# Expert choice one step every other unit, the count at unit 100, scatters two units apart from unit 116

## The chip, the cores and the metric

The kernel runs on one core of one Trainium2 chip. The metric is the device time of one execution in microseconds. TensorE (PE), VectorE (DVE), ScalarE (ACT) and GpSimd (POOL) work side by side and wait for each other through semaphores; SyncE (SP) issues most transfers.

## The reference, cut to what matters

Sixteen images of 128 channels by 1024 positions go through an attention layer and a mixture-of-experts layer:

```
x = x + attention(layernorm_over_channels(x))      # 8 heads of 16, 1024 x 1024 scores per head
t = tokens(x)                                      # 16 x 1024 tokens of 128
t = t + experts(layernorm(t))                      # 16 experts, 128 -> 512 -> 128, two per token
```

The gating takes, per token, a softmax over 16 logits and the two largest gates with their experts. An expert takes at most 256 tokens of an image by its first mask and, behind those, tokens of the second mask. This needs a running count of tokens per expert over the image (`cumsum`) and gives every token two places in the experts' lists. Each chosen token is scaled by its gate and summed.

## The kernel before, in words

**Two phases.** The first runs over the 16 images (the code's batches, `B`): attention, and for the image before it the projection, the residual, the layer norm, the gating and the scatter of its rows, sorted by expert, to `sorted_rows` in memory. The second runs over 136 x 2 blocks of 128 sorted rows: the experts. Only the first is touched here.

**Units.** A batch is 128 units (`SLOTS`), each one 128 x 512 tile of exponentials, in four stages of 32 (`UNITS`). In unit `u` PE makes a tile of scores for the maxima of unit `u + 45` (`max_unit`, L1405, matmul L1415), then the tile of scores of unit `u` (`score_unit`, L1429, matmul L1439). At u mod 32 = 2, 7, 10, 14, 18, 22, 26 and 30 it also weighs the values with four tiles of exponentials (`weigh`, L1443, eight matmul records of L1456). DVE reduces the first tile to its row maxima (`take_max`, L946, L952), ACT takes the exponentials of the second (L795). Both kinds of tile have three buffers (`RING = 3`), so that PE is at most three tiles ahead of DVE and of ACT.

**Side work** is written out by unit number in each engine's program; an engine runs its program in order. DVE: `divide` in units 4 to 7 of each stage (L977), norm statistics in units 8 to 17 and 24 to 32, residual additions at 13 and 17, the start of the gating at 38 (`choose`), and then `choose_experts` (L1040), a generator of 22 steps: one is taken after `take_max` of each unit from 44 on, left out where u mod 32 is in `BUSY` (3 to 7 and 18 to 21). So before the change the steps stand in units 44 to 49, 54 to 66 and 72 to 74. The twentieth step also writes `masks_b` (L1103), which PE's `count_tokens` (L1484, 16 small matmuls) waits for. PE counts at unit 77 and ACT copies the counts at unit 78 (`copy_counts`, L845).

**POOL** runs, in this order within batch b: the last scatters of image b-2, with `place_v(b, 1)` (L584) behind the first of them; `normalise_x(b+1)` (L567), whose result PE needs for `project_qk` (L1391) at unit 33; `normalise_tokens(b-1)`; `split_qk`, `place_v(b+1, 0)` and `add_bias`; `place_rows(b-1)` (L615), which waits for the counts and for all 22 steps of the choice; and the first scatters of image b-1 (`scatter`, L721, one indirect transfer of 128 rows, L732, which waits for the score tile of its unit).

Of the kernel before, what the change touches and what calls it, by code (L numbers as in the profile page):

```python
# [25 lines left out]
UNITS = TB * HG  # L26
# [6 lines left out]
BUSY = (3, 4, 5, 6, 7, 18, 19, 20, 21)  # L33
# [66 lines left out]
def metaformer(nc, x, wq, wk, wv, wproj, bproj, wgate, w1, w2, out):  # L100
    ctx = ExitStack()
    with ctx:
# [34 lines left out]
        at = 0  # L137
# [374 lines left out]
        def _(gp):  # L512
# [227 lines left out]

            def batch(b, first, last):
                at = SLOTS * b
                rest = range(8, 16) if b > 1 else range(0)
                for n in rest[:1]:
                    scatter(b - 2, n, at + 1)
                place_v(b, 1)
                for n in rest[1:5]:
                    scatter(b - 2, n, at + 4 * (n - 8) + 1)
                if not last:
                    normalise_x(b + 1)  # L750
                for n in rest[5:]:
                    scatter(b - 2, n, at + 4 * (n - 8) + 1)
                if not first:
                    normalise_tokens(b - 1)
                if not last:
                    for i in range(4):
                        split_qk(b + 1, i)
                    place_v(b + 1, 0)
                add_bias(b)
                if not first:  # L760
                    place_rows(b - 1)
                    if b == EARLY:
                        keep_counts()
                    for n in range(16 if last else 8):
                        scatter(b - 1, n, at + 96 + (2 if last else 4) * n)

            for b in range(B):
                batch(b, b == 0, b == B - 1)
# [20 lines left out]
        def _(act):  # L789
# [68 lines left out]
            def batch(b, first, last):  # L858
                for u in range(SLOTS):
                    exp_unit(b, u)  # L860
                    if not last:
                        if u == 2:
                            copy_xt(b + 1, 0)
                        if u == 6:
                            copy_xt(b + 1, 1)
                        if u == 33:
                            copy_qk(b + 1, 0)
                        if u == 42:
                            copy_qk(b + 1, 1)
                        if u == 45:  # L870
                            copy_qk(b + 1, 2)
                        if u == 49:
                            copy_qk(b + 1, 3)
                        if u == 52:
                            copy_v(b + 1, 0)
                        if u == 55:
                            copy_v(b + 1, 1)
                    if not first:
                        if u == 21:
                            copy_tokens(b - 1, 0)  # L880
                        if u == 23:
                            copy_tokens(b - 1, 1)
                        if u == 41:
                            gate_exponentials(b - 1)
                        if u in (74, 82):
                            copy_rows(b - 1, (u - 74) // 8)
                        if u == 78:
                            copy_counts(b - 1)
                    if u % UNITS == MSLOT + 1 and not (last and u > 96):
                        copy_m(b, u // UNITS + 1)  # L890
# [54 lines left out]
        def _(dve):  # L945
# [215 lines left out]
            def batch(b, first, last):  # L1161
                for u in range(SLOTS):
# [14 lines left out]
                    if not first:  # L1177
# [10 lines left out]

                        if u == 44:
                            choice = choose_experts(b - 1)  # L1190
                        if u >= 44 and u % UNITS not in BUSY:
                            next(choice, None)

            batch(0, True, False)
# [180 lines left out]
        def _(pe):  # L1375
# [138 lines left out]
            def batch(b, first, last):  # L1514
                freed[0] = (m_copied, STAGES * b + 1)
                for u in range(SLOTS):
# [25 lines left out]
                    if not first:  # L1542
# [7 lines left out]
                            transpose_tokens(b - 1, 1)  # L1550
                        if u == 36:
                            logits(b - 1)
                        if u == 77:
                            count_tokens(b - 1)
                    if u % UNITS == MSLOT and not (last and u > 96):
                        rows_of_maxima(b, u // UNITS + 1)
# [106 lines left out]
```

## Time and profile before

| | us |
|---|---|
| three runs | 2384.68, 2387.88, 2392.95 |
| median | 2387.88 |
| profiled execution, its own time | 2377.1 |
| its span, first to last instruction | 2375.2 |
| first phase, 16 batches, ends near | 1741 |
| a batch, from unit 0 to unit 0 | 104.9 to 106.5 |

The engines' busy shares are over the whole span, and the first phase is where the change is. A reader finds the time of a unit by counting the records of L952 (DVE) or L795 (ACT): record 128 b + u of L795 is unit u of batch b, and record 128 b + u + 45 of L952. For batch 6, which the rows are taken from, this gives the start of DVE's unit 44 at 731.9 us, 58 at 745.6, 67 at 752.6, 72 at 756.7, 80 at 763.0, 100 at 776.7, 107 at 782.5 and 112 at 785.8, and ACT's unit 0 at 691.9 and of the next batch at 796.8. A line of a timeline can merge neighbours (x4: four in a row, with their time from the first start to the last end).

### The profile page before, as it was taken

The page shows a single profiled execution, that of the slowest core. Times are in us where ns is not written, and L with a number is a line of the kernel's source. Part 1 is how long each engine was busy: PE and PEld are TensorE (multiplying, and loading weights), DVE is VectorE, ACT ScalarE, POOL GpSimd, SP SyncE. Part 2 cuts the span into 40 slices and gives each one's busy share as a digit, 9 for nine tenths or more (in the row PEclk, how much of TensorE's full clock was granted, in tenths as well). Part 3 has the DMA queues.
Part 4 walks back from the last instruction along what each step waited for, and adds up shares of the span by engine and source line. Part 5 has one row for each costly group of instructions (what it writes and reads, how often), then busy time and mean ns, then how long its engine had stood idle before and what let it go on. Part 6 is the DMA issues. An engine that isn't in the chain of part 4 may idle for free. (4 is left out here: it accounts for less than half of the span.)

```text
span 2375.2 us, 49241 instructions
## 1 busy us (share of the span) xinstructions
PE 2119.9 (89%) x14610; PEld 1161.0 (49%) x14610; DVE 1846.1 (78%) x4351; ACT 1542.5 (65%) x3153; POOL 1041.2 (44%) x1630
## 2 busy tenths in 40 slices
PE   6999999898999999899999999999846999999994
PEld 3333333333333333333333333333326999999994
DVE  6898989989998999999899998999733554445573
ACT  1677777767677777767777777777723665556551
POOL 3204544443444445344444434444344555555542
PEclk9999999999999999999999999999968999999997
DMA  4223323132323323232332313223052222222684
GB/s 121 46 41 59 62 49 72 35 66 48 64 57 57 68 41 68 41 63 53 65 62 49 70 36 65 54 53 63 17 181 72 70 70 67 67 70 70 177 248 133
DMA packets 134693, 170.57 MB, mean 72 GB/s; under 512 B 31118, under 2 KB 101140, under 8 KB 134450
## 3 DMA queue, kind: packets, MB, share of 16 engines
q1 hardware_dynamic: 117618, 134.24, 26.4%
q0 software_dynamic: 16896, 34.12, 4.1%
q8 instruction: 90, 1.47, 0.3%
q14 instruction: 89, 0.73, 0.1%
HBM read 64.86 MB, written 48.86 MB: 48 GB/s over the span
## 5 line engine op out<-in xcount | busy, mean ns | idle before, releaser
L952 DVE TENSOR_REDUCE sb_m_red<-banks 128x1 f32<-128x512 f32 x2048 | 1325.9, 678 | 152.4 <-PE banks L1415 144.1
L795 ACT ACTIVATE sb_arena_a<-banks 128x512 f32<-128x512 f32 x2048 | 1115.3, 599 | 446.4 <-PE banks L1439 406.8
L1415 PE MATMUL banks<-sb_arena_b 62*128 62x512 f32 x2048 | 814.4, 467 | 105.1 <-DVE sb_m_red L952 91.2
L1439 PE MATMUL banks<-sb_arena_b 64*128 64x512 f32 x2048 | 806.4, 462 | 10.7 <-ACT sb_arena_a L795 5.7
L1415 PEld LDWEIGHTS banks<-sb_arena_b 62*128 62x128 f32 x2048 | 346.9, 187 | 769.8 <-DVE sb_m_red L952 637.3
L1456 PE MATMUL banks<-sb_arena_a,sb_arena_d 128*32 128x512 f32 x4096 | 550.7, 610 | 10.0 <-ACT sb_arena_a L795 4.2
L732 POOL DMA_INDIRECT sorted_rows<-sb_rows,sb_place x256 | 251.2, 981 | 341.3 <-PE banks L1439 306.2
L778 POOL DMA_INDIRECT expert_out<-sb_arena_d x272 | 274.2, 1008 | 268.5 <-DVE sb_arena_d L1321 178.6
L1439 PEld LDWEIGHTS banks<-sb_arena_b 64*128 64x128 f32 x2048 | 337.8, 185 | 32.0 <-ACT sb_arena_a L795 24.6
L1584 PE MATMUL banks<-sb_arena_d,sb_arena_c 128*128 128x128 f32 x2176 | 289.4, 276 | 1.3 <-ACT sb_arena_d L908 1.3
L1593 PE MATMUL banks<-sb_arena_c 128*128 128x128 f32 x2176 | 287.9, 275 | 2.6 <-ACT sb_arena_c L915 1.7
L1314 DVE COPY sb_arena_c<-sb_arena_b 128x512 f32 x272 | 141.0, 518 | 173.1 <-issue 95.5
L1584 PEld LDWEIGHTS banks<-sb_arena_d,sb_arena_c 128*128 128x128 f32 x2176 | 265.9, 193 | 2.2 <-issue 1.7
L1593 PEld LDWEIGHTS banks<-sb_arena_c 128*128 128x128 f32 x2176 | 264.8, 192 | 3.7 <-issue 2.8
L915 ACT ACTIVATE sb_arena_c<-banks 128x512 f32<-128x512 f32 x272 | 162.5, 598 | 108.4 <-PE banks L1584 95.9
L1311 DVE COPY sb_arena_c<-sb_arena_a 128x512 f32 x272 | 114.2, 420 | 88.5 <-PE banks L1584 55.0
L922 ACT ACTIVATE sb_arena_d<-banks,sb_arena_d 128x128 f32<-128x128 f32 x272 | 100.1, 368 | 108.4 <-issue 55.0
L1456 PEld LDWEIGHTS banks<-sb_arena_a,sb_arena_d 128*32 128x32 f32 x4096 | 80.8, 108 | 155.0 <-issue 73.6
L588 POOL TENSOR_SCALAR sb_arena_d<-sb_v_st 128x512 f32<-128x512 f32 x32 | 19.8, 619 | 272.9 <-PE banks L1456 256.2
L1576 PE MATMUL banks<-sb_ident,sb_arena_d 128*128 128x128 f32 x272 | 74.7, 274 | 32.2 <-DMA sb_arena_d<-sorted_rows 32.2
L908 ACT ACTIVATE sb_arena_d<-banks 128x128 f32<-128x128 f32 x272 | 74.1, 272 | 42.8 <-PE banks L1576 39.4
L1395 PE MATMUL banks<-sb_xt,sb_wq_r 128*128 128x512 f32 x128 | 76.0, 677 | 10.2 <-POOL sb_xt L570 8.1
(185 smaller groups left out, 1617.3 us busy)
## 6 DMA issues: line engine op xcount, KB each, us to landing
sb_arena_b<-sb_arena_c SPq DMA_DIRECT2D x768, 64.0 KB, 2.3
sb_arena_d<-sorted_rows SPq DMA_DIRECT2D x272, 66.0 KB
sb_x_in<-in_x_dram SPq DMA_DIRECT2D x16, 512.0 KB, 3.8
sb_res<-in_x_dram SPq DMA_DIRECT2D x16, 512.0 KB, 3.6
sb_x_all<-sb_res SPq DMA_DIRECT2D x16, 512.0 KB, 3.1
expert_out<-sb_arena_d POOLq DMA_INDIRECT x272
sorted_rows<-sb_rows,sb_place POOLq DMA_INDIRECT x256
sb_arena_a<-in_L_ffn_w_dram SPq DMA_DIRECT2D x1, 4096.0 KB, 14.0
```

The costliest lines, as they stand in the source:

```text
L732: nc.gpsimd.indirect_dma_start(out=sorted_rows[:, :], out_offset=bass.IndirectOffsetOnAxis(ap=place[:, k, j:j + 1], axis=0), in_=rows[:, k ...
L778: nc.gpsimd.indirect_dma_start(out=expert_out[:, :], out_offset=bass.IndirectOffsetOnAxis(ap=blk_dest[:, s % WR:s % WR + 1], axis=0), in_= ...
L795: nc.scalar.activation(probs[:, u % PRING, :], ps_score[:, u % RING, :], ACT.Exp, scale=SCALE).then_inc(exp_done, 1)
L915: nc.scalar.activation(hid[:, s % 2, :], ps_h[:, s % 2, :], ACT.Relu).then_inc(hid_done, 1)
L952: nc.vector.tensor_reduce(out=m_red[:, s % 2, at:at + 1], in_=ps_max[:, m % SLOTS % RING, :], axis=AX.X, op=ALU.max).then_inc(max_taken, 1)
L1311: nc.vector.tensor_copy(w1_blk[:, s % WR, :], w1_all[:, bass.ds(e, 1), :].rearrange("p a h -> p (a h)")).then_inc(w1_copied, 1)
L1314: nc.vector.tensor_copy(w2_blk[:, s % WR, :], w2_all[:, bass.ds(e, 1), :, :].rearrange("p a c d -> p (a c d)")).then_inc(w2_copied, 1)
L1415: nc.tensor.matmul(ps_max[:, m % SLOTS % RING, :], qs[rows_of, g, l, half * HALF + t * P:half * HALF + (t + 1) * P], ks[rows_of, g, l, kh ...
L1439: nc.tensor.matmul(ps_score[:, u % RING, :], ks[rows_of, g, l, i * P:(i + 1) * P], qs[rows_of, g, l, half * HALF:(half + 1) * HALF], start ...
L1456: last = nc.tensor.matmul(ps_pv[32 * h:32 * h + 32, :], v_pad[:, i, HG * g + h, :], probs[:, (4 * n + h) % PRING, :], start=(i == 0), stop ...
L1584: last = nc.tensor.matmul(ps_h[:, s % 2, c * P:(c + 1) * P], w1_blk[:, s % WR, c * P:(c + 1) * P], blk_xt[:, s % 2, :], start=True, stop=True)
L1593: last = nc.tensor.matmul(ps_o[s % WR], hid[:, s % 2, c * P:(c + 1) * P], w2_blk[:, s % WR, c * P:(c + 1) * P], start=(c == 0), stop=(c == ...
```

## The change

The choice takes one step in odd units alone: 45, 47, 49, 55, 57, 59, 61, 63, 65, 73, 75, 77, 79, 81, 87, 89, 91, 93, 95, 97, 105 and 107, the twentieth at 97. The count moves to unit 100 on PE and its copy to 101 on ACT. Of an image's 16 scatters six instead of eight are written behind `place_rows`, from unit 116 on two units apart (before: eight from 96 on, four apart), and ten in the next batch in units 1 to 19, two apart (before: eight in units 1 to 29, four apart); all ten now stand before `normalise_x`, of which before three stood behind it. The last batch keeps its choice in every unit, its count at 77 and its sixteen scatters from 96.

```diff
-                rest = range(8, 16) if b > 1 else range(0)
+                rest = range(6, 16) if b > 1 else range(0)
                 for n in rest[:1]:
                     scatter(b - 2, n, at + 1)
                 place_v(b, 1)
-                for n in rest[1:5]:
-                    scatter(b - 2, n, at + 4 * (n - 8) + 1)
+                for n in rest[1:]:
+                    scatter(b - 2, n, at + 2 * (n - 6) + 1)
                 if not last:
                     normalise_x(b + 1)
-                for n in rest[5:]:
-                    scatter(b - 2, n, at + 4 * (n - 8) + 1)
...
-                    for n in range(16 if last else 8):
-                        scatter(b - 1, n, at + 96 + (2 if last else 4) * n)
+                    for n in range(16 if last else 6):
+                        scatter(b - 1, n, at + (96 if last else 116) + 2 * n)
...
-                        if u == 78:
+                        if u == (78 if last else 101):
                             copy_counts(b - 1)
...
-                        if u >= 44 and u % UNITS not in BUSY:
+                        if u >= 44 and (u % 2 or last) and u % UNITS not in BUSY:
                             next(choice, None)
...
-                        if u == 77:
+                        if u == (77 if last else 100):
                             count_tokens(b - 1)
```

## Rows read from the trace of the kernel before

**Rows 1.** The page's line of busy times.

```profile
PE 2119.9 (89%) x14610; PEld 1161.0 (49%) x14610; DVE 1846.1 (78%) x4351; ACT 1542.5 (65%) x3153; POOL 1041.2 (44%) x1630
```

**Rows 2.** Windows: stretch, length, busy us of PE, PEld, DVE, ACT, POOL, granted clock.

```profile
269.50:375.40 105.90, 97.28 (x616) 38.17 (x616) 96.04 (x216) 77.04 (x147) 47.97 (x86) 0.98 0.29 57
587.10:692.00 104.90, 95.88 (x616) 37.79 (x616) 96.09 (x216) 77.14 (x147) 47.99 (x86) 1.00 0.28 57
...
303.10:306.40 3.30, 3.30 (x16) 0.99 (x14) 3.05 (x8) 1.57 (x3) 3.22 (x7) 0.50 0.52 166
```

**Rows 3.** Windows of batch 6: units 44 to 57, 58 to 66, 72 to 79, 80 to 99.

```profile
731.90:745.60 13.70, 12.73 (x84) 5.29 (x82) 11.28 (x28) 9.76 (x20) 4.95 (x5) 1.00 0.00 1
745.60:752.60 7.00, 6.18 (x42) 2.28 (x38) 7.00 (x19) 5.21 (x11) 0.51 (x1) 1.00 0.18 30
...
756.70:763.00 6.30, 6.03 (x48) 2.54 (x48) 5.37 (x13) 4.78 (x11) 0.76 (x2) 1.00 0.40 68
763.00:776.70 13.70, 12.56 (x84) 4.48 (x84) 12.67 (x24) 11.43 (x24) 10.22 (x37) 1.00 0.29 49
```

**Rows 4.** Timeline of DVE, batch 6, units 59 and 60, then the steps of 65 and 66.

```profile
746.46 0.69 DVE L952 TENSOR_REDUCE sb_m_red<-banks 128x1 f32<-128x512 f32 x1
747.07 0.28 DVE L1067 TENSOR_TENSOR sb_tmp<-sb_gat,sb_small 128x128 f32<-128x128 f32 x1
747.27 0.68 DVE L952 TENSOR_REDUCE sb_m_red<-banks 128x1 f32<-128x512 f32 x1
...
751.67 0.16 DVE L1097 TENSOR_TENSOR sb_masks<-sb_masks,sb_small 128x8 f32<-128x8 f32 x1
...
752.35 0.38 DVE L1100 TENSOR_TENSOR sb_masks<-sb_masks,sb_small 128x8 f32<-128x8 f32 x1
```

**Rows 5.** Timeline of DVE from unit 111: no choice there; in brackets idle time, releaser.

```profile
785.25 2.48 DVE L952 TENSOR_REDUCE sb_m_red<-banks 128x1 f32<-128x512 f32 x4 [0.22 <-PE banks L1415]
...
793.53 2.48 DVE L952 TENSOR_REDUCE sb_m_red<-banks 128x1 f32<-128x512 f32 x4 [0.38 <-PE banks L1415]
```

**Rows 6.** Timeline of PE over the same units.

```profile
786.00 0.49 PE L1415 MATMUL banks<-sb_arena_b 62*128 62x512 f32 x1 [0.30 <-DVE sb_m_red L952]
...
786.42 1.06 PE L1456 MATMUL banks<-sb_arena_a,sb_arena_d 128*32 128x512 f32 x8
...
788.70 0.50 PE L1415 MATMUL banks<-sb_arena_b 62*128 62x512 f32 x1 [0.30 <-DVE sb_m_red L952]
```

**Rows 7.** Timeline of PE around the count at unit 77.

```profile
759.02 0.49 PE L1415 MATMUL banks<-sb_arena_b 62*128 62x512 f32 x1
...
760.49 0.50 PE L1415 MATMUL banks<-sb_arena_b 62*128 62x512 f32 x1
```

**Rows 8.** Timeline of DVE, units 78 and 79, behind that count.

```profile
761.03 0.69 DVE L952 TENSOR_REDUCE sb_m_red<-banks 128x1 f32<-128x512 f32 x1 [0.20 <-PE banks L1415]
762.45 1.29 DVE L952 TENSOR_REDUCE sb_m_red<-banks 128x1 f32<-128x512 f32 x2 [0.73 <-PE banks L1415]
```

**Rows 9.** Timeline: PE's scores of units 100 and 101, then DVE's maximum of unit 101.

```profile
775.93 0.61 PE L1415 MATMUL banks<-sb_arena_b 62*128 62x512 f32 x2
...
777.96 0.65 DVE L952 TENSOR_REDUCE sb_m_red<-banks 128x1 f32<-128x512 f32 x1
```

**Rows 10.** Timeline of POOL: first and last of the 36 instructions of `place_rows`.

```profile
762.16 0.46 POOL L635 TENSOR_TENSOR sb_tmp<-sb_counts,sb_masks 128x128 f32<-128x128 f32 x1 [7.10 <-ACT sb_counts L848]
...
774.28 0.20 POOL L676 CAST sb_place<-sb_small 128x16 int32<-128x16 f32 x1
```

**Rows 11.** Timeline of POOL: first and last of sixteen scatters with nothing between them.

```profile
1775.63 1.11 POOL L732 DMA_INDIRECT sorted_rows<-sb_rows,sb_place  x1 [0.54 <-POOL sb_place L718]
...
1795.10 0.96 POOL L732 DMA_INDIRECT sorted_rows<-sb_rows,sb_place  x1 [0.30 <-issue]
```

**Rows 12.** Timeline, batch 6: `normalise_x` on POOL, then the first `project_qk` on PE.

```profile
708.47 0.20 POOL L558 TENSOR_SCALAR sb_ln_var<-sb_mean_var 128x8 f32<-128x8 f32 x1 [1.56 <-DVE sb_mean_var L1005]
...
710.82 3.48 POOL L570 TENSOR_SCALAR sb_xt<-sb_xt,sb_neg_mean,sb_rstd 128x128 f32<-128x128 f32 x8
...
720.21 1.12 PE L1395 MATMUL banks<-sb_xt,sb_wq_r 128*128 128x512 f32 x2
```

## The prediction

> **What bounds the kernel now.** First read the line of busy times [rows 1]: PE 89% and DVE 78% over the span. These are averages over two phases, and the change touches only the attention phase, so the windows of whole batches come next [rows 2]. In a batch of 104.90 us PE is busy 95.88 and DVE 96.09. Neither is the bound alone: both have about 9 us of idle time, not at the same places. The question is where a DVE step lies beside a busy PE (it is free) and where beside an idle one (it costs).
>
> The windows by units answer it [rows 3]. In units 44 to 57 DVE is busy 11.28 of 13.70 us and PE 12.73: PE has the projections of the next image there, and DVE waits for it. In units 58 to 66 DVE is busy 7.00 of 7.00 us and PE 6.18: DVE is the bound, with a choice step in every unit. In units 72 to 79 DVE is busy 5.37 of 6.30 and PE 6.03: the count stops DVE. In units 80 to 99 DVE is busy 12.67 of 13.70.
>
> The timeline gives the prices. Back to back, the maxima come 0.60 us apart: four in 2.48 us with 0.68 for the last [rows 4, 5], (2.48 - 0.68) / 3 = 0.60. With one step of 0.28 us between, they come 747.27 - 746.46 = 0.81 us apart, since neighbours overlap [rows 4]. So such a step costs DVE 0.20. Where there are no steps, four units still take 788.70 - 786.00 = 2.70 us, not 2.40 [rows 6]. That is a loop: PE makes a tile, DVE reduces it, that frees one of three buffers, PE makes a tile (0.49), weighs (1.06) and only then makes the next. Once per four units PE waits 0.30 for DVE [rows 6] and DVE waits 0.22 for PE [rows 5]. DVE's work in a group is 0.69 + 3 x 0.60 = 2.49, so 0.21 is spare, and 0.09 more comes back when DVE no longer waits (its first maximum then takes 0.60, not 0.69). One step of 0.20 in four units is free. Two make 2.40 + 0.40 = 2.80 us, 0.10 above the loop. Four make 3.20, 0.50 above it. This is the whole case for spreading: a steeper price for dense steps.
>
> **Units 44 to 57, five steps fewer.** PE is the bound; a lighter DVE waits longer for the same tiles. Gain 0. The cover is PE's 12.73 busy us in 13.70 [rows 3].
>
> **Units 58 to 66, nine steps become four.** Now 7.00 us [rows 3]. After: unit 58 without a step 0.60, units 59 to 62 with two steps 2.80, units 63 to 66 with two, one of them smaller, 2.74. Sum 6.14, 0.86 less. But DVE now reaches unit 67, behind the weighing of unit 66, without arrears and meets the wait of the loop, 0.22 + 0.09 = 0.3. Gain 0.56, say 0.6; bounds 0.3 (the wait is as long as the 0.38 of another group [rows 5] and the groups take 2.9) and 0.9 (no wait). Here the profile also shows two engines in each other's way: the step L1100 takes 0.38 us beside POOL's `place_v`, while L1097, of the same shape, takes 0.16 [rows 4]. The step moves to unit 95, where POOL is idle; its 0.2 is within the 0.6. The Trainium skill (GPSIMD Engine Reference, Specifications) says that GpSimd shares its SBUF interfaces with VectorE and contends with DVE instructions that have two SBUF inputs, and the trace agrees, with these 0.38 and 0.16 us. By that rule `place_rows`, now beside units 107 to 126, could slow other DVE steps; they are few and I add nothing.
>
> **Units 72 to 79, three steps become four and the count leaves.** Now 6.30 to 6.38 us. Behind the count DVE waits 0.20 and 0.73 [rows 8]. After, four steps on eight units: 8 x 0.60 + 4 x 0.20 = 5.60. Gain 0.75; bounds 0.5 (one wait of the loop stays) and 0.8.
>
> **Units 80 to 107, nine steps come in.** Steps of 0.20 at 81 and 87, 0.14 at 89, 0.08 at 91, 93, 95 and 105, about 0.34 at 97 (with the cast for the count) and 0.10 at 107: 1.3 us of DVE time. There are five groups up to 99, one weighing each, with 0.31 spare each, and 0.31 in the last group before 112. By groups only 84 to 87 is over, by 0.1 to 0.15. Cost 0.15; bounds 0 and 1.3 (nothing is hidden).
>
> **The count at unit 100.** It holds up PE: the next tile comes 760.49 - 759.02 = 1.47 us after the last instead of some 0.4, so it costs PE about 1.05 us [rows 7]. At unit 100 DVE starts the four steps of `divide`. PE's tile of unit 100 starts at 775.93; with the count behind it the next would start at 777.40 and be done at 777.89, and DVE asks for it at 777.96 [rows 9]. So the count is just covered, by the transpose that DVE makes before. ACT's copy of 0.5 us behind it sits in an engine that is busy 77 of 105 us [rows 2]. The masks are written at DVE's unit 97, before PE may be at 100 (three buffers). Cost 0; bounds 0 and 0.93, what DVE waits behind it now [rows 8]. I take 0 because the times above say so, without much to spare.
>
> **POOL and what is queued behind its waits.** `place_rows` waits for the 22nd step, now in unit 107 at 782.6 + 0.2, instead of at 762.16; it takes 774.48 - 762.16 = 12.3 us [rows 10] and ends at about 795.1, that is 1.7 us before the next unit 0 at 796.8 and 10 units behind unit 116. So the scatters will not follow the written spacing: they run back to back. Sixteen such take (1795.10 - 1775.63) / 15 = 1.30 us each [rows 11]. From 795.7 on (a start 0.5 to 0.8 behind) they take 16 x 1.30 = 20.8, with `place_v` (0.8) between: to 817.3, or 20.5 us behind unit 0. Only then `normalise_x` starts, which takes 710.82 + 3.48 - 708.47 = 5.8 us [rows 12]: ready at 26.3 us. PE asks for it at 720.21 - 691.9 = 28.3 us [rows 12]. It is covered, with 2.0 us to spare where there were 5.9. `place_v(b, 1)` is late by 6 us for a use at unit 71. The first `project_qk`, the tiles behind it on PE, and through them DVE and ACT, all wait if that margin goes. SP's queue waits for none of these.
>
> **The sum.** 0.6 + 0.75 - 0.15 - 0 = 1.2 us a batch. The choice is changed in 14 batches (1 to 14): 14 x 1.2 = 16.8 us. The profiled execution, 2377.1 us, would take 2360.3. It is 10.8 us under the median of the runs shown; the same 16.8 off the median 2387.88 gives 2371.1. Bounds of the terms: best 0.9 + 0.8 = 1.7 a batch, 24 us, 2364; the ordinary bad side 0.3 + 0.6 - 0.4 = 0.5 a batch, 7 us, 2381.
>
> **Rivals.**
> (a) The steps cost what they take and the count is not covered. The 9 steps cost, say, 0.7 instead of 0.15 and the count gives back 0.5: 0.6 + 0.75 - 0.7 - 0.5 = 0.15 a batch, 2 us, 2386. For it: the cover of the count is 0.07 us by the rows. Against it: 0.31 spare per group is measured, and behind unit 103 DVE is behind anyway.
> (b) POOL is late. If the scatters beside running attention take more than 1.30 + 2.0 / 16 = 1.43 us each, or `place_rows` starts 2 us later, PE stops at unit 33 in every batch, and all of the lateness is lost, since PE is the bound there. From 3.2 us of lateness (a scatter of 1.50 us) the gain is gone; at 1.6 us a scatter, 4.8 us late, 2.8 are lost: 14 x (2.8 - 1.2) = 22 us slower, 2410. For it: one spacing in the middle of the phase, right behind `place_rows`, was 1.4. Against it: the other close ones were 1.3, as in the tail.
> (c) The clock. TensorE's granted clock fell to half (1.2 GHz) five times in the phase, as at 303.1 [rows 2], each time in units 35 to 38, behind small matmuls of the logits among waits; such a batch took 105.9 instead of 104.9. PE then does the same kind of work at 100 (small count matmuls, then waits for DVE). If the clock fell there in each batch, 14 x 1.0 = 14 us would eat the gain: 2385. The Trainium skill (TensorE: Matmul & The Clock Gate, Part 1) says that the clock is gated by how busy PE has been; at unit 77, where the count is now, no fall is seen.
> (d) The written spacing of scatters does nothing, since POOL runs behind it (above). That is part of the forecast, not against it.
>
> **How the numbers follow.** Forecast 2371, its own range 2362 to 2381, chance 0.72. (a) 0.14, (c) 0.04, both about no change; (b) 0.10, of which 0.07 slower by over 0.3% and 0.03 a smaller loss. The range for 8 in 10 takes in part of (a) and (c): 2362 to 2387. 0.3% is 7.2 us, about what a measurement of this kernel tells from no change: faster 0.73, same 0.18, slower 0.09.
>
> **What would show it.** In the profile after: batches of 103.7 us; units 58 to 66 in about 6.2 us and 72 to 79 in about 5.6; units 80 to 99 no longer than 13.9; no DVE wait over 0.3 behind the count; the sixteen scatters back to back with `normalise_x` ending near 26 us after unit 0 and no wait of L1395 for it. A wait of L1395 for POOL, or a DVE wait of 0.5 or more at unit 101, would make me wrong.

## The result and the profile after

The change made the kernel slower. The median of four runs is 2492.73 us (2490.30 to 2494.37), the kernel before beside it 2388.08 (2384.68 to 2392.95, four runs); the ratio is 1.0447 with a 95% interval of 1.0421 to 1.0474. The profiled execution took 2493.6 us, its span is 2491.7. The forecast was 2371, faster. Of the experiments below, two executions of v2_dense (3240 and 4672 us) and one of x1_rows16 (6675 us) took far longer than the rest for a reason that no profile shows; their figures leave these out.

Lines of the text from L760 on stand two lower than in the kernel before: the maximum is L950, its matmul L1413, the scores L1437, the weighing L1454, the exponentials L793. In the kernels with added transfers on GpSimd the maximum is L967 and the scores L1454.

The page after; under the busy line the fortieths of the span, for TensorE's granted clock in tenths. It answers to [rows 1].

```profile
span 2491.7 us, 49241 instructions
...
PE 2187.5 (88%) x14610; PEld 1182.8 (47%) x14610; DVE 1835.9 (74%) x4351; ACT 1533.1 (62%) x3153; POOL 1037.8 (42%) x1630
...
PEclk9999899999989998989999999989876999999997
```

PE is 68 us busier with the same 14610 matmuls, and the clock, which in the kernel before fell to half five times for 3.4 us in the attention phase, now falls near the head of every batch from batch 2 on, for 6.8 to 13.7 us. That says that something is different in each batch, not what.

Windows of after (stretch, length, busy us of PE, PEld, DVE, ACT, POOL, granted clock): batch 5 whole, then of batch 6 the units 0 to 15, 44 to 57, 58 to 66, 72 to 79 and 80 to 99. They answer to [rows 2, 3].

```profile
606.90:718.30 111.40, 98.52 (x616) 38.49 (x616) 95.79 (x215) 76.90 (x148) 47.65 (x86) 0.95 0.26 54
...
718.40:741.80 23.40, 18.33 (x85) 7.63 (x86) 14.08 (x31) 10.03 (x19) 14.20 (x16) 0.71 0.37 76
...
767.00:780.70 13.70, 12.73 (x84) 5.29 (x82) 10.13 (x23) 9.76 (x20) 4.96 (x5) 1.00 0.01 1
780.70:787.10 6.40, 5.99 (x40) 2.03 (x36) 6.23 (x14) 4.93 (x10) 0.29 (x1) 1.00 0.14 24
791.10:796.80 5.70, 5.18 (x34) 1.68 (x34) 5.67 (x13) 4.61 (x10) 0.00 (x0) 1.00 0.45 76
796.80:810.50 13.70, 13.01 (x87) 4.59 (x88) 13.59 (x32) 11.37 (x23) 0.00 (x0) 1.00 0.29 49
```

The same units 0 to 15 in the kernel before:

```profile
692.00:706.60 14.60, 13.61 (x85) 5.92 (x86) 13.53 (x31) 10.41 (x20) 5.01 (x6) 1.00 0.43 75
```

Every window that the forecast spoke of came out near it: 7.00 became 6.40, 6.30 became 5.70, 13.70 stayed 13.70. The loss is in units 0 to 15, which it did not price: 14.60 became 23.40. Of these 8.8 us, 4.1 are more idle time of PE (5.07 against 0.99) and 4.7 more busy time, at a clock of 0.71. DVE and ACT do the same work in more time. Over batches 2 to 13 the mean is 14.6 before and 23.1 after; a batch takes 112.7 instead of 105.3, and 14 times 7.4 (batches 2 to 15) is 104 us, the whole difference.

Now the timelines of that stretch in batch 6, whose unit 0 is at 718.4. First POOL; between the second line shown and the `place_v` at 726.78 stand five more scatters, 1.26 us apart.

```profile
718.06 1.11 POOL L732 DMA_INDIRECT sorted_rows<-sb_rows,sb_place  x1 [0.80 <-issue]
719.48 0.97 POOL L732 DMA_INDIRECT sorted_rows<-sb_rows,sb_place  x1 [0.30 <-issue]
...
726.78 0.63 POOL L588 TENSOR_SCALAR sb_arena_d<-sb_v_st 128x512 f32<-128x512 f32 x1
727.60 0.99 POOL L732 DMA_INDIRECT sorted_rows<-sb_rows,sb_place  x1 [0.18 <-remote]
728.90 0.95 POOL L732 DMA_INDIRECT sorted_rows<-sb_rows,sb_place  x1 [0.30 <-issue]
732.16 0.95 POOL L732 DMA_INDIRECT sorted_rows<-sb_rows,sb_place  x1 [2.31 <-remote]
```

Then DVE, PE and ACT.

```profile
719.99 0.69 DVE L950 TENSOR_REDUCE sb_m_red<-banks 128x1 f32<-128x512 f32 x1 [0.34 <-PE banks L1413]
721.41 0.69 DVE L950 TENSOR_REDUCE sb_m_red<-banks 128x1 f32<-128x512 f32 x1 [0.73 <-issue]
723.84 0.69 DVE L950 TENSOR_REDUCE sb_m_red<-banks 128x1 f32<-128x512 f32 x1 [1.73 <-PE banks L1413]
...
726.08 0.69 DVE L950 TENSOR_REDUCE sb_m_red<-banks 128x1 f32<-128x512 f32 x1 [0.93 <-PE banks L1413]
...
731.88 0.69 DVE L950 TENSOR_REDUCE sb_m_red<-banks 128x1 f32<-128x512 f32 x1 [4.96 <-remote]
```

```profile
721.22 0.63 PE L1413 MATMUL banks<-sb_arena_b 62*128 62x512 f32 x2
...
722.37 0.50 PE L1413 MATMUL banks<-sb_arena_b 62*128 62x512 f32 x1
...
724.58 0.79 PE L1413 MATMUL banks<-sb_arena_b 62*128 62x512 f32 x1 [1.14 <-DVE sb_m_red L950]
...
727.78 0.79 PE L1413 MATMUL banks<-sb_arena_b 62*128 62x512 f32 x1
...
732.63 0.79 PE L1413 MATMUL banks<-sb_arena_b 62*128 62x512 f32 x1 [3.67 <-issue]
```

```profile
727.51 0.60 ACT L793 ACTIVATE sb_arena_a<-banks 128x512 f32<-128x512 f32 x1 [2.37 <-remote]
731.92 0.60 ACT L793 ACTIVATE sb_arena_a<-banks 128x512 f32<-128x512 f32 x1 [3.81 <-remote]
```

DVE is idle though PE's tiles are recorded long before. PE's three tiles from 721.22 to 722.87 are taken at 723.84, 726.08 and 731.88: the last is 9.0 us late. ACT waits at the same times for the other kind of tile. The packed trace also records steps of the semaphore that PE raises for DVE, though not every one: the last before these three starts are at 723.81, 726.05 and 731.86, each within 0.03 us of the start. So DVE starts as soon as its signal is there, and it is the signal that comes late. It is a circle: PE has three buffers and can't go on until DVE frees one, so PE waits as well (1.14, 3.67), its clock falls, and a tile of 0.50 takes 0.79. The longer waits of DVE begin at the fourth scatter (722.1) and behind the seventh (726.9), and the engines go on some two us after the run pauses at 729.85, because POOL itself then waits for the score tile of a unit that is held up (2.31). "remote" as a releaser means that a semaphore step is recorded where the wait ends, but no instruction's record ends near it; "issue" means that not even a step is shown. Here "remote" is the sign that a signal came later than the work it stands for.

So the sixteen scatters do not run back to back from first to last. In batch 6 nine follow each other closely, with `place_v` between the seventh and the eighth; then the engines that they held up make POOL itself wait, and the last ends at 744.19, 26.1 us behind the start of the first. The pattern is the same in each batch from 2 to 15, with nine to twelve close ones.

### The profile page after: what moved, and what is told of

It is laid out like the page before. It is cut to its first block and busy times, and to the rows that moved or that the text cites. A ratio compares the mean times of both kernels' runs of the same rounds, so it can differ in the third digit from the quotient of the medians.

```text
span 2491.7 us, 49241 instructions
## 1 busy us (share of the span) xinstructions
PE 2187.5 (88%) x14610; PEld 1182.8 (47%) x14610; DVE 1835.9 (74%) x4351; ACT 1533.1 (62%) x3153; POOL 1037.8 (42%) x1630
## 3 DMA queue, kind: packets, MB, share of 16 engines
q0 software_dynamic: 16896, 34.12, 3.9%
q8 instruction: 90, 1.47, 0.2%
## 5 line engine op out<-in xcount | busy, mean ns | idle before, releaser
L950 DVE TENSOR_REDUCE sb_m_red<-banks 128x1 f32<-128x512 f32 x2048 | 1331.4, 679 | 252.2 <-PE banks L1413 169.9
L793 ACT ACTIVATE sb_arena_a<-banks 128x512 f32<-128x512 f32 x2048 | 1113.6, 599 | 559.0 <-PE banks L1437 442.7
L1413 PE MATMUL banks<-sb_arena_b 62*128 62x512 f32 x2048 | 830.5, 477 | 141.8 <-DVE sb_m_red L950 103.7
L1437 PE MATMUL banks<-sb_arena_b 64*128 64x512 f32 x2048 | 824.9, 474 | 22.3 <-issue 11.2
L1413 PEld LDWEIGHTS banks<-sb_arena_b 62*128 62x128 f32 x2048 | 352.7, 192 | 825.2 <-DVE sb_m_red L950 655.8
L1454 PE MATMUL banks<-sb_arena_a,sb_arena_d 128*32 128x512 f32 x4096 | 570.3, 630 | 5.1 <-ACT sb_arena_a L793 1.7
L1437 PEld LDWEIGHTS banks<-sb_arena_b 64*128 64x128 f32 x2048 | 343.8, 190 | 56.2 <-ACT sb_arena_a L793 32.6
L1312 DVE COPY sb_arena_c<-sb_arena_b 128x512 f32 x272 | 131.4, 483 | 187.8 <-PE banks L1591 128.8
L635 POOL TENSOR_TENSOR sb_tmp<-sb_counts,sb_masks 128x128 f32<-128x128 f32 x15 | 6.9, 457 | 414.2 <-DVE sb_small L1110 387.3
L1454 PEld LDWEIGHTS banks<-sb_arena_a,sb_arena_d 128*32 128x32 f32 x4096 | 81.8, 109 | 155.0 <-issue 78.4
L588 POOL TENSOR_SCALAR sb_arena_d<-sb_v_st 128x512 f32<-128x512 f32 x32 | 20.1, 629 | 242.0 <-PE banks L1454 224.8
```

The lines of the kernel that those rows point to most:

```text
L793: nc.scalar.activation(probs[:, u % PRING, :], ps_score[:, u % RING, :], ACT.Exp, scale=SCALE).then_inc(exp_done, 1)
L950: nc.vector.tensor_reduce(out=m_red[:, s % 2, at:at + 1], in_=ps_max[:, m % SLOTS % RING, :], axis=AX.X, op=ALU.max).then_inc(max_taken, 1)
L1312: nc.vector.tensor_copy(w2_blk[:, s % WR, :], w2_all[:, bass.ds(e, 1), :, :].rearrange("p a c d -> p (a c d)")).then_inc(w2_copied, 1)
L1413: nc.tensor.matmul(ps_max[:, m % SLOTS % RING, :], qs[rows_of, g, l, half * HALF + t * P:half * HALF + (t + 1) * P], ks[rows_of, g, l, kh ...
L1437: nc.tensor.matmul(ps_score[:, u % RING, :], ks[rows_of, g, l, i * P:(i + 1) * P], qs[rows_of, g, l, half * HALF:(half + 1) * HALF], start ...
L1454: last = nc.tensor.matmul(ps_pv[32 * h:32 * h + 32, :], v_pad[:, i, HG * g + h, :], probs[:, (4 * n + h) % PRING, :], start=(i == 0), stop ...
```

## The experiments

What follows separates the theories: that the dense run of scatters as such holds PE up (in the expectations, theory D, for density), or its place (P), the choice and the count (C), the bytes in memory (Y), GpSimd's making of descriptors, the records that tell the DMA engines what to move (G), or the form of the transfer. The gain or loss by stretch is the mean over batches 2 to 13 of DVE's time by units, against the kernel before.

### One half of the change at a time

**s1_spacing**, the new places of the scatters with the old choice and count:

```diff
-                rest = range(8, 16) if b > 1 else range(0)
+                rest = range(6, 16) if b > 1 else range(0)
...
-                for n in rest[1:5]:
-                    scatter(b - 2, n, at + 4 * (n - 8) + 1)
+                for n in rest[1:]:
+                    scatter(b - 2, n, at + 2 * (n - 6) + 1)
...
-                for n in rest[5:]:
-                    scatter(b - 2, n, at + 4 * (n - 8) + 1)
...
-                    for n in range(16 if last else 8):
-                        scatter(b - 1, n, at + 96 + (2 if last else 4) * n)
+                    for n in range(16 if last else 6):
+                        scatter(b - 1, n, at + (96 if last else 116) + 2 * n)
```

> The kernel before with the scatter edit alone: six from unit 116 and ten in units 1 to 19, two units apart, with the choice and the count where they were. Place_rows ends at unit 97, so the scatters follow their units: 1.36 us apart before unit 0 and 1.7 us behind it, not back to back. Theory D (scatters back to back for more than some 5 us hold up PE): little or no stall, 2380 to 2400 us. Theory P (any dense scatters in units 1 to 12, where the stack moves and the transposes lie, hold up PE): a stall of several us a batch, 2450 us or more. Theory C (the moved choice and count do it): 2388 us.

Measured: 2408.73 us against 2379.28, ratio 1.0126 (1.0063 to 1.0189). The scatters are on time here, yet units 120 to 127 take 1.2 us more, 0 to 7 1.15 and 8 to 15 0.35. Two units apart is some 1.8 us on average, but in bursts of up to six neighbours at 1.3. So the written spacing of two alone costs 1%, less than a third of the loss. That is more than theory D allowed for (2400 at most) and far below theory P's 2450.

**s3_choice**, the new choice, count and copy with the scatters where the kernel before has them; against the changed kernel:

```diff
-                rest = range(6, 16) if b > 1 else range(0)
+                rest = range(8, 16) if b > 1 else range(0)
...
-                for n in rest[1:]:
-                    scatter(b - 2, n, at + 2 * (n - 6) + 1)
+                for n in rest[1:5]:
+                    scatter(b - 2, n, at + 4 * (n - 8) + 1)
...
+                for n in rest[5:]:
+                    scatter(b - 2, n, at + 4 * (n - 8) + 1)
...
-                    for n in range(16 if last else 6):
-                        scatter(b - 1, n, at + (96 if last else 116) + 2 * n)
+                    for n in range(16 if last else 8):
+                        scatter(b - 1, n, at + 96 + (2 if last else 4) * n)
```

> The changed kernel with the scatter schedule of before. Place_rows still ends near unit 126, so eight scatters run back to back from there to about unit 9, and eight follow four units apart. Theory D: a part of the stall, 2 to 4 us a batch, less 1.2 us that the choice gains: 2400 to 2430 us. Theory P: about the same as D. Theory C: 2490 us.

Measured: 2479.34 us against 2379.28, ratio 1.0423 (1.0361 to 1.0484). The late choice alone brings nearly the whole loss, since eight scatters that were written from unit 96 on find `place_rows` unfinished and are caught up on in one run across unit 0. Units 0 to 15 take 8.8 us more; units 56 to 63, 64 to 71 and 72 to 79 take 0.33, 0.32 and 0.70 less, as in the full change. Theory D's range, 2400 to 2430, was missed, and theory C's 2490 came nearer; the next two runs and v1_spread decide between them. Theory D had counted on half the scatters and so on a part of the stall. But nine run closely here (in batch 6 from 716.62 to 727.85), as many as in the same batch of the changed kernel.

### The same sixteen scatters in one run, elsewhere

**s2_burst_head**: old choice and count, and all sixteen back to back around unit 0; they wait for unit 127 and for unit 1.

```diff
-                rest = range(8, 16) if b > 1 else range(0)
+                rest = range(6, 16) if b > 1 else range(0)
...
-                for n in rest[1:5]:
-                    scatter(b - 2, n, at + 4 * (n - 8) + 1)
+                for n in rest[1:]:
+                    scatter(b - 2, n, at + 1)
...
-                for n in rest[5:]:
-                    scatter(b - 2, n, at + 4 * (n - 8) + 1)
...
-                    for n in range(16 if last else 8):
-                        scatter(b - 1, n, at + 96 + (2 if last else 4) * n)
+                    for n in range(16 if last else 6):
+                        scatter(b - 1, n, at + (96 + 2 * n if last else 127))
```

> The kernel before, choice and count where they were, with the scatters made back to back by hand: six wait for unit 127, ten for unit 1. Theory D and theory P: the stall of the changed kernel, 8 us a batch, 2490 to 2510 us. Theory C: 2388 us.

Measured: 2572.33 us against 2379.28, ratio 1.0814 (1.0748 to 1.0880): units 0 to 15 take 13.6 us more, nothing else changes. The choice and the count aren't needed for the loss. Here no unit's signal paces the run, all sixteen come closely, and it costs more than in the changed kernel, and more than the 2490 to 2510 expected.

**s4_burst_mid**: all sixteen right behind `place_rows`, none in the next batch.

```diff
-                rest = range(8, 16) if b > 1 else range(0)
+                rest = range(0)
...
-                    for n in range(16 if last else 8):
-                        scatter(b - 1, n, at + 96 + (2 if last else 4) * n)
+                    for n in range(16):
+                        scatter(b - 1, n, at + (96 + 2 * n if last else 97))
```

> The kernel before with all sixteen scatters back to back right behind place_rows, units 97 to 127, and none in the next batch. There are few stack moves and no transposes of x there. Theory D: a stall of about 8 us a batch, 2490 us or more. Theory P: no stall, 2380 to 2390 us. Theory C: 2388 us.

Measured: 2552.77 us against 2379.28, ratio 1.0732 (1.0665 to 1.0798). The head of the batch is as before, and units 104 to 119 take 12.4 us more. So it isn't the neighbourhood of unit 0, with its loads and transposes. DVE, PE and the last scatter on POOL, of that run in batch 6; the scatters start at 832.28.

```profile
841.54 1.44 DVE L952 TENSOR_REDUCE sb_m_red<-banks 128x1 f32<-128x512 f32 x2 [1.85 <-PE banks L1415]
843.67 1.43 DVE L952 TENSOR_REDUCE sb_m_red<-banks 128x1 f32<-128x512 f32 x2 [0.69 <-PE banks L1415]
853.53 0.69 DVE L952 TENSOR_REDUCE sb_m_red<-banks 128x1 f32<-128x512 f32 x1 [8.43 <-remote]
```

```profile
846.09 1.05 PE L1415 MATMUL banks<-sb_arena_b 62*128 62x512 f32 x2
...
846.51 0.74 PE L1439 MATMUL banks<-sb_arena_b 64*128 64x512 f32 x1
854.28 0.79 PE L1415 MATMUL banks<-sb_arena_b 62*128 62x512 f32 x1 [7.03 <-DVE sb_m_red L952]
```

```profile
851.37 0.96 POOL L732 DMA_INDIRECT sorted_rows<-sb_rows,sb_place  x1 [0.30 <-issue]
```

DVE is idle for 8.43 us with tiles of PE recorded at 846.09 to 847.14 in front of it, and goes on 1.2 us after the last scatter ends (852.33). PE, with its buffers full, starts nothing for 7.03 us behind these records, and then 0.06 us after DVE's maximum ends (854.22).

### Eight scatters more, for nothing

The next runs add eight transfers per batch to the kernel before, in batches 0 to 14, from unit 52 on, where POOL is idle. They write a constant to a tensor that nobody reads. **d1_full** adds indirect ones of 128 rows of 528 bytes (`extras(b)` is called on POOL behind `split_qk`; `extra_at` holds fixed row numbers):

```diff
+            def extras(b):
+
+                wait(gp, extra, 16 * 8 * b)
+                for n in range(8):
+                    wait(gp, scores_ready, SLOTS * b + 52 + 0 * n)
+                    nc.gpsimd.indirect_dma_start(
+                        out=scratch[:, :], out_offset=bass.IndirectOffsetOnAxis(ap=extra_at[:, n:n + 1], axis=0),
+                        in_=pad_row[:, :], in_offset=None).then_inc(extra, 16)
```

> The kernel before plus eight extra scatters of 128 rows of 528 bytes each, back to back on GpSimd from unit 52 of each of the 15 first batches, to a scratch tensor; nothing else moves. GpSimd is idle there (units 53 to 66). Theory D (back-to-back scatters hold up PE, whatever else runs): 4 to 9 us a batch, 60 to 135 us more, 2440 to 2515 us. If the stall needs the kernel's own scatters or their place: 2380 to 2390 us.

Measured: 2430.99 us against 2383.94, ratio 1.0197 (1.0167 to 1.0226): 47 us for 15 runs of eight, 3.1 us each, in units 56 to 71. POOL and DVE of batch 6:

```profile
757.42 1.07 POOL L746 DMA_INDIRECT scratch<-sb_pad_row,sb_extra_at  x1 [0.17 <-issue]
758.80 0.96 POOL L746 DMA_INDIRECT scratch<-sb_pad_row,sb_extra_at  x1 [0.30 <-issue]
...
766.38 0.96 POOL L746 DMA_INDIRECT scratch<-sb_pad_row,sb_extra_at  x1 [0.31 <-issue]
```

```profile
763.28 0.68 DVE L967 TENSOR_REDUCE sb_m_red<-banks 128x1 f32<-128x512 f32 x1
...
766.12 0.69 DVE L967 TENSOR_REDUCE sb_m_red<-banks 128x1 f32<-128x512 f32 x1 [1.96 <-remote]
```

The wait begins 6.7 us behind the start of the run, at the sixth scatter, in a part of the batch in which the kernel before has no scatter. Nothing that runs there needs the transfers or waits for them: this is the disputed cost by itself. It is smaller than expected (2440 at least).

**d2_small**: the same with 4 bytes a row.

```diff
-                        in_=pad_row[:, :], in_offset=None).then_inc(extra, 16)
+                        in_=pad_row[:, 0:1], in_offset=None).then_inc(extra, 16)
```

> As d1_full, but each extra scatter writes 4 bytes a row instead of 528: the same number of descriptors made by GpSimd, 1/132 of the bytes. Theory G (GpSimd's making of descriptors holds up PE): as slow as d1_full. Theory Y (the bytes do it): no slower than before.

Measured: 2440.05 us against 2383.94, ratio 1.0235 (1.0177 to 1.0293). Less than a hundredth of the bytes, and no less of a loss. It isn't bandwidth.

**d4_sync**: the bytes and rows of d1_full as plain transfers, issued by SyncE.

```diff
+                wait(sp, extra, 16 * 8 * b)
+                for n in range(8):
+                    wait(sp, scores_ready, SLOTS * b + 52 + 0 * n)
+                    sp.dma_start(scratch[n * P:(n + 1) * P, :], pad_row[:, :]).then_inc(extra, 16)
```

> As d1_full, but the eight transfers of 128 rows of 528 bytes are plain ones, issued by SyncE: the same bytes and rows in the same stretch without GpSimd. Theory G: 2380 to 2395 us. Theory Y: as slow as d1_full.

Measured: 2381.39 us against 2383.94, ratio 0.9996 (0.9980 to 1.0012). Nothing, though SyncE issues the eight within 3.65 us in batch 6.

**d3_direct**: the same plain transfers, issued by GpSimd.

```diff
-                    nc.gpsimd.indirect_dma_start(
-                        out=scratch[:, :], out_offset=bass.IndirectOffsetOnAxis(ap=extra_at[:, n:n + 1], axis=0),
-                        in_=pad_row[:, :], in_offset=None).then_inc(extra, 16)
+                    nc.gpsimd.dma_start(scratch[n * P:(n + 1) * P, :], pad_row[:, :]).then_inc(extra, 16)
```

> As d1_full, but the eight transfers on GpSimd are plain ones of 128 rows of 528 bytes, without row addresses. If it is any transfer whose descriptors GpSimd makes: 2420 us or more. If it is the indirect form: 2380 to 2395 us.

Measured: 2382.71 us against 2380.29, ratio 1.0023 (1.0009 to 1.0037). In the profile, that of the fastest of eight executions, no stretch differs by more than 0.1 us a batch; the 0.2% of the times has no place there. The transfers come faster than the indirect ones, eight in 4.42 us:

```profile
736.93 4.42 POOL L746 DMA_DIRECT2D scratch<-sb_pad_row  x8
```

The profiles count the same packets on GpSimd's DMA queue here as in d1_full (20736 against 16896 before) and the same bytes. Eight transfers in close order on GpSimd's queue don't bring the stall when they are plain ones. That points to the indirect form, but a rival stands: this run is over in 4.42 us, while DVE's first long wait begins 4.0 us (the change) to 6.7 us (d1_full) behind the start of a run. Plain transfers in a run of 10 us or more were not tried.

**x1_rows16**: d1_full with 16 rows in each scatter instead of 128.

```diff
-                        out=scratch[:, :], out_offset=bass.IndirectOffsetOnAxis(ap=extra_at[:, n:n + 1], axis=0),
-                        in_=pad_row[:, :], in_offset=None).then_inc(extra, 16)
+                        out=scratch[:, :], out_offset=bass.IndirectOffsetOnAxis(ap=extra_at[0:16, n:n + 1], axis=0),
+                        in_=pad_row[0:16, :], in_offset=None).then_inc(extra, 16)
```

> As d1_full, but each of the eight extra indirect scatters moves 16 rows of 528 bytes from 16 partitions instead of 128 rows: an eighth of the row addresses and of the descriptors. If the stall comes with the instruction (reading addresses on GpSimd, whatever their number), as slow as d1_full, 2431 us. If it comes with the number of rows made into descriptors: 2380 to 2395 us.

Measured: the profiled execution took 2463.27 us against 2380.51, and units 56 to 63 5.7 us more. It is the only usable execution, so there is no interval. POOL, then DVE, of batch 6:

```profile
773.96 0.85 POOL L746 DMA_INDIRECT scratch<-sb_pad_row,sb_extra_at  x1 [0.30 <-PE banks L1454]
775.11 0.83 POOL L746 DMA_INDIRECT scratch<-sb_pad_row,sb_extra_at  x1 [0.30 <-issue]
```

```profile
780.73 0.69 DVE L967 TENSOR_REDUCE sb_m_red<-banks 128x1 f32<-128x512 f32 x1 [3.32 <-remote]
...
783.53 0.69 DVE L967 TENSOR_REDUCE sb_m_red<-banks 128x1 f32<-128x512 f32 x1 [1.91 <-remote]
```

With an eighth of the rows a scatter still takes 0.83 us, they follow at 1.15 instead of 1.27, and the wait is longer (3.32 against 1.96). As far as one execution tells, the cost hangs on the number of instructions in a row and their pace, and not on the rows.

### How many, and how close

**t1_two_apart**: the eight of d1_full, two units apart.

```diff
-                    wait(gp, scores_ready, SLOTS * b + 52 + 0 * n)
+                    wait(gp, scores_ready, SLOTS * b + 52 + 2 * n)
```

> As d1_full, but the eight extra scatters wait for units 52, 54, up to 66: two units apart, some 1.7 us instead of 1.27. The same eight scatters, POOL's place_v and add_bias behind them later by a few us. Theory R (what counts is the rate over several scatters): 2380 to 2395 us. If it is their number: as slow as d1_full, 2431 us.

Measured: 2386.56 us against 2380.29, ratio 1.0030 (0.9985 to 1.0076); units 64 to 71 take 0.2 us more, the rest nothing. The distances on POOL are 1.3 to 2.2 us, 1.6 on average:

```profile
743.10 0.96 POOL L746 DMA_INDIRECT scratch<-sb_pad_row,sb_extra_at  x1 [0.30 <-issue]
744.80 0.96 POOL L746 DMA_INDIRECT scratch<-sb_pad_row,sb_extra_at  x1 [0.74 <-PE banks L1454]
747.03 0.96 POOL L746 DMA_INDIRECT scratch<-sb_pad_row,sb_extra_at  x1 [1.27 <-PE banks L1454]
```

**t2_four**: four of them, back to back.

```diff
-                wait(gp, extra, 16 * 8 * b)
-                for n in range(8):
+                wait(gp, extra, 16 * 4 * b)
+                for n in range(4):
```

> As d1_full with four extra scatters instead of eight, back to back. In the profiles the first stall of DVE comes 6 us or more behind the start of a run, at its fifth or sixth scatter. If the stall builds up over a run: little or nothing, 2380 to 2395 us. If each scatter costs its share: half of d1_full's loss, 2405 us.

Measured: 2387.93 us against 2380.29, ratio 1.0030 (1.0017 to 1.0044). No stretch of the profile differs by more than 0.05 us a batch, but the profiled execution, 2380.00 us, was the fastest of eight; the 0.3% of the times has no place in it, and stays unexplained. Eight at 1.27 us cost 3.1 us, four at the same pace no visible stall, eight at 1.6 on average hardly one.

Set beside each other, the runs of t2_four, d1_full, s4_burst_mid and s2_burst_head last 4.9, 9.9, 20.1 and 20.9 us from their first start to their last end in batch 6, and cost 0, 3.2, 12.4 and 13.6 us a batch. So with 128 rows a run costs about what it lasts beyond some 7 us. That is an estimate from these four, and s3_choice doesn't fit it: its run lasts 11.2 us and units 0 to 15 lose 8.8. Whether the scatters that follow that run explain this isn't shown.

### The gain without the loss

If density is the cause, the change's other half must give its 1.2 us a batch as soon as the scatters are spread. **v1_spread** keeps the choice, the count and the copy of the change, and writes the sixteen scatters into the next batch, never closer than three units; the normalisation of the rows, which overwrites their source, goes behind them, and `copy_rows` from units 74 and 82 to 96 and 112. The last batch stays as before. In the diff, `some` takes the next scatters in order and lets each wait for its unit.

```diff
+                some((1,))
                 place_v(b, 1)
-                for n in rest[1:5]:
-                    scatter(b - 2, n, at + 4 * (n - 8) + 1)
+                some((5, 9, 13, 17))
...
+                    some((22, 26, 30))
...
+                    some((37,))
...
+                    some((52, 55, 58, 61, 64))
...
+                    some((71, 74))
+                    if not first:
+                        normalise_rows(b - 1)
...
-                    for n in range(16 if last else 8):
-                        scatter(b - 1, n, at + 96 + (2 if last else 4) * n)
+                    for k in range(16 if last else 0):
+                        scatter(b - 1, k, at + 96 + 2 * k)
```

> The changed kernel's choice, count and copy, with no two scatters closer than three units: sixteen in the next batch at units 1, 5, 9, 13, 17, 22, 26, 30, 37, 52, 55, 58, 61, 64, 71 and 74; to allow it the rows' normalisation stands behind the last of them and the copies of rows at units 96 and 112 (the last batch keeps the order of before). Theory D with the gain of the choice as forecast, 1.2 us a batch: 2360 to 2368 us beside 2380 of before. If the choice or the count itself costs: 2380 us or more.

Measured: 2362.01 us against 2383.94, ratio 0.9907 (0.9879 to 0.9936). Its windows of units 0 to 15, 58 to 66, 72 to 79 and 80 to 99:

```profile
681.70:696.30 14.60, 13.56 (x84) 5.89 (x85) 13.52 (x31) 10.38 (x21) 5.26 (x6) 1.00 0.42 75
735.40:741.80 6.40, 5.98 (x40) 2.04 (x36) 6.23 (x15) 4.92 (x11) 2.67 (x4) 1.00 0.26 55
745.80:751.50 5.70, 5.25 (x34) 1.74 (x34) 5.68 (x13) 4.10 (x9) 2.34 (x5) 1.00 0.53 99
751.50:765.20 13.70, 13.03 (x88) 4.58 (x88) 13.61 (x33) 11.37 (x23) 2.13 (x5) 1.00 0.30 49
```

Unit for unit these are the changed kernel's times where that gained, and the old 14.60 where it lost. The batch is 103.93 us, 1.38 less than before. Written three units apart, the scatters still come in pairs at 1.3 to 1.4 us, about three a batch, where POOL had other work before them; three in a row are rare.

**v1_again** is the same kernel on another chip.

> v1_spread once more beside x1_rows16, in three rounds, for an interval of the version without dense scatters: 2358 to 2366 us beside 2380 of before, a ratio of 0.990 to 0.993.

Measured: 2363.55 us (2360.23 to 2369.00) against 2380.51, ratio 0.9927 (0.9911 to 0.9944).

**v2_dense** is v1_spread with the choice in every unit again, the count left at 100:

```diff
-                        if u >= 44 and (u % 2 or last) and u % UNITS not in BUSY:
+                        if u >= 44 and u % UNITS not in BUSY:
```

> v1_spread with the choice in every unit again, as before the change, the count still at unit 100 and the scatters as in v1_spread. By the terms of the prediction the batch gives back 0.6 us in units 58 to 66 and keeps most of the 0.75 us of units 72 to 79 (the count is gone from there): 0.45 to 0.6 us a batch slower than v1_spread, 2366 to 2372 us. If the spread steps make the whole gain: 2380 us.

Measured: 2375.47 us against 2380.29, ratio 0.9977 (0.9959 to 0.9995), slower than the 2366 to 2372 expected. By stretches it gains 0.63 us in units 72 to 79 and loses 0.16 in 96 to 103, and units 56 to 71 are as before. The moved scatters and copies are in this kernel too, so the 0.63 is put down to the count only because it stood there. So of v1_spread's 0.7 to 0.9%, the larger part comes from the spread choice, and a quarter to a third from the moved count.

## Why the prediction was wrong

**The step that failed** is the part "POOL and what is queued behind its waits". It foresaw the event: `place_rows` ends just before unit 0, and the scatters "run back to back". It priced them as a delay of POOL's own queue alone. The price in a close run, 1.30 us each, is right (1.27 measured), and the question asked of it, whether `normalise_x` is late, has the right answer too, though the sixteen with `place_v` took 26.1 us and not 21.6. What it took for granted is that a run of scatters leaves the other engines alone, a term that it put at nothing without naming it. The rows it read for them, [rows 11], come from the tail of the phase, where PE has nothing to do (0.00 us busy from 1775.60 to 1796.10): they can show what a scatter costs POOL, and can't show what it costs PE. The missing term is 8.5 us a batch (units 0 to 15, 14.6 to 23.1) against a gain of 1.2.

**Rival (d)** held this very consequence, that POOL runs behind the written spacing, and set it down as "part of the forecast, not against it". It was the whole loss: s3_choice has it without the new spacing and s2_burst_head without the choice. What the sentence had wrong is not the lateness but that nothing hangs on it.

**Rival (b)** looked at the right instructions with the wrong mechanism. Its conditions weren't met: `normalise_x` starts at 744.26, 25.9 us behind unit 0, and ends at 750.06, 31.7 behind, but all units are late by more than that, and the first projections wait for POOL no longer than before. Its 2410 would have come from PE stopping at unit 33; PE stopped at units 1 to 15.

```profile
744.26 0.20 POOL L558 TENSOR_SCALAR sb_ln_var<-sb_mean_var 128x8 f32<-128x8 f32 x1
...
746.60 3.46 POOL L570 TENSOR_SCALAR sb_xt<-sb_xt,sb_neg_mean,sb_rstd 128x128 f32<-128x128 f32 x8
```

**Rival (c)**, the clock: it fell in every batch, but from units 3 to 11 on and behind PE's waits, not behind the count at 100. Where the stall is gone, this fall is gone too (v1_spread's windows show 1.00), so it follows from the stall. In batch 6, 4.7 of the 8.8 us are busy time at the lower clock; how much shorter the stall would be at the full clock isn't shown.

**Units 44 to 57**, gain 0: right, 13.70 with DVE at 10.13 instead of 11.28 [rows 3].

**Units 58 to 66**, 0.6 within 0.3 to 0.9: right. Batch 6 gives 7.00 to 6.40, the mean of units 56 to 71 is 0.64 less.

**Units 72 to 79**, 0.75 within 0.5 to 0.8: batch 6 gives 0.60, the mean 0.71.

**Units 80 to 107**, cost 0.15: 0.05 in the change, 0.07 in v1_spread. The loop's spare time hides nine steps nearly whole.

**The count at unit 100**, cost 0 by a cover of 0.07 us: right, and so rival (a) is out. DVE's maximum of unit 101 follows the transpose without a wait, and PE's gap from tile to tile is 1.38 us (810.98 - 809.60) against the 1.47 of [rows 7]. DVE, then PE:

```profile
811.12 0.70 DVE L982 STREAM_TRANSPOSE sb_o_t<-banks 128x512 f32<-128x512 f32 x1
811.75 0.65 DVE L950 TENSOR_REDUCE sb_m_red<-banks 128x1 f32<-128x512 f32 x1
```

```profile
809.60 0.40 PE L1413 MATMUL banks<-sb_arena_b 62*128 62x512 f32 x1
...
810.98 0.49 PE L1413 MATMUL banks<-sb_arena_b 62*128 62x512 f32 x1
```

**The sum**, 1.2 us a batch, was right for what it counted: v1_spread gains 1.38 and v1_again 1.25, in units 56 to 107 alone 1.24 and 1.30, and their 2362.01 and 2363.55 lie in the likeliest case's own range of 2362 to 2381. The range of the forecast failed since the bounds were taken around each term on DVE and PE, and none around "what sixteen scatters do to the rest".

## What to carry to other kernels

When a producer moves later, look at what was spaced out behind it: its written spacing becomes one run, and the run is a new load that no row of the profile before may show. A row priced where the other engines are idle bounds what an instruction costs its own queue, not what it costs its neighbours; give that term a bound of its own, or measure it with a few copies that do nothing. In this kernel indirect scatters of GpSimd cost nothing beside a busy TensorE as long as only two, rarely three, come within 1.5 us of each other, as in v1_spread; bursts of up to six cost s1_spacing 1%.

## What the runs showed of the hardware

**Indirect scatters in a close run hold TensorE's results up.** Sixteen, 1.27 us apart, cost 12.4 us (s4_burst_mid) and 13.6 (s2_burst_head); nine, with others behind them, 8.5 (the change) and 8.8 (s3_choice); eight 3.1 (d1_full); eight of 16 rows, 1.15 apart, 6.0 in one execution (x1_rows16); four cost no visible stall, and eight at 1.6 us on average hardly any. DVE's first wait over 1.5 us begins at the fourth scatter (the change) to the sixth (d1_full, s4_burst_mid). The stall appears in three places of the batch, and stays with 4 bytes a row instead of 528; eight plain transfers of GpSimd in 4.42 us or of SyncE show nothing in their profiles. DVE and ACT wait for PE's tiles up to 9 us behind their records, while PE takes up DVE's signals at once (731.88 + 0.69 = 732.57, PE's next tile at 732.63). The long wait ends 1.2 us (s4_burst_mid) and 2.0 us (the change) behind the last scatter of the run.

**What stays open** is the mechanism. The ends of matmuls are modelled in the trace, so whether PE's matmuls run late or only their signals can't be told. Nor is the resource known. The Trainium skill (DMA: Bandwidth & Descriptors, SWDGE vs HWDGE vs iDMA) says that GpSimd builds the descriptors of all its transfers in software and writes them to rings in SBUF, while SyncE's are made by hardware. If the making of descriptors alone did it, the plain transfers of d3_direct should disturb as well. Eight of them don't, but their run of 4.42 us is shorter than any that showed the stall (t2_four, 4.9 us, shows none either), so this speaks against it without ruling it out, and no run here shows what the indirect form does beyond it.

**A scatter's price hardly hangs on its size:** 0.96 us on POOL and 0.30 to the next with 128 rows, 0.83 and 0.30 with 16, and 0.55 us in all for a plain transfer of the same bytes (4.42 / 8).
